# Attention passes and MLP of a transformer block written out as one list of ticks, with the row maxima placed by DMA

## The chip, the core and the metric

The kernel runs on one core of one Trainium2 chip. Five engines work side by side: TensorE (PE, matmuls into PSUM; its weight loads are shown apart as PEld), VectorE (DVE), ScalarE (ACT), GpSimd (POOL) and SyncE (SP), which issues all of the kernel's transfers. The metric is the device time in microseconds (us) from the first to the last instruction.

## The reference

Two cross-attention layers and one MLP, all in float32, over 8 batches of 512 rows and 512 columns, with 16 heads of 32 columns. The first layer's result of batch 0 is added to every batch.

```python
# layer 0
att = softmax(q @ k.T / sqrt(32)) @ v      # q of x, k and v of ctx
x = x + att[0]                             # batch 0's attention for all batches
# layer 1, for each batch
q = layer_norm(x) @ Wq;  k, v = layer_norm(ctx) @ Wkv
x = x + softmax(q @ k.T * SCALE) @ v @ Wproj + bproj
x = x + gelu(layer_norm(x) @ W1 + b1) @ W2 + b2     # hidden width 2048
```

So there are 9 attention passes: pass 0 for layer 0 (batch 0 alone) and passes 1 to 8 for the batches of layer 1.

## The kernel before

Every float32 operand of a product is held as two parts (hi and lo, in the fast type fp32r), and each product is three matmuls: hi by hi, hi by lo, lo by hi. A projected tile of 128 x 512 (a "unit") is so 12 matmuls of 512 columns for its 4 chunks of the inner dimension.

An attention pass is 64 quarters (`CH`): 16 heads, 4 chunks of 128 rows each. In quarter k the PE makes the scores of chunk k with queries as rows (`ps_s`, L587), DVE takes their row maxima (L993), and 6 quarters later (`SHIFT_LAG`) PE makes the same scores again with keys as rows (`ps_t`, L602), now with a 97th inner row that holds minus the maxima, so that they come out shifted. ACT takes the exponential twice (L806 as the hi part, L812 whole), DVE subtracts for the lo part (L999; chunk 2 of each head on POOL, L1175), and 8 quarters after the first scores (`WEIGH_LAG`) PE multiplies both parts with the values (`ps_o`, L622). The three operands of a head lie one above the other in `q_st` and `k_st`; SP stacks them with 4 transfers per head (`load_stack`, L376) and lays the head's result into place with 2 (`place_head`, L391 and L392).

How the maxima come into the 97th row of `q_st`: once a head has its 4 columns of maxima, PE spreads them with 4 small matmuls against an identity (L634), and ACT copies one row of 512 (L799):

```python
for c in range(TC):
    ins = nc.tensor.matmul(ps_m[0:KM, c * P:c * P + P],
                           negmax[:, h % 2, c:c + 1].broadcast_to([P, KM]), id_r[:], ...)
act.activation(q_st[KQ:KM, h % G], ps_m[KQ:KM], ACT.Identity).then_inc(m_moved, 1)
```

Between these, `PLAN` puts the parts of other units by quarter: the values, keys and queries of the passes next, the output projection of the pass before, the transposes of the layer norms. Passes 0, 1 and 8 are written out (`FIRST`, `COLD`, `LAST`), passes 2 to 7 are a hardware loop on every engine. When all passes are through, the MLP runs by itself, batch by batch (`tile`): hidden units (L696), Gelu twice from PSUM (L880, L881), the subtraction on DVE (L1063), and the second product (L710), which adds up over all 16 hidden units in four PSUM banks. Its weights stay in SBUF, where the attention's tiles were; the rows between the two parts go through DRAM (`x2_scratch`).

Of the kernel before, what the change touches and what calls it, by code (L numbers as in the profile page):

```python
# [11 lines left out]
P = 128  # L27
# [28 lines left out]
POOL_CHUNK = 2
STACK_AHEAD = 6  # L60

EARLY = TC
TURN_AT = 12
# [5 lines left out]
PLAN = [  # L69
    (("v", 0), 0, (4, 4, 5, 5)), (("v", 1), 1, (5, 6, 6, 6)), (("v", 2), 0, (7, 7, 7, 8)),  # L70
    (("v", 3), 1, (8, 8, 9, 9)), (("q", 1), 0, (10, 10, 11, 11)), (("k", 2), 1, (12, 13, 14, 15)),
    (("out", 0), 0, (16, 17, 17, 18)), (("out", 1), 1, (18, 19, 20, 20)), (("q", 2), 0, (21, 22, 23, 23)),
# [6 lines left out]
]  # L79


def plus(a, b):

    return a + b if b >= 0 else a - (-b)


class Pass:


    def __init__(self, n, kind="steady"):  # L90
        self.n = n
        self.first, self.cold, self.last = kind == "first", kind == "cold", kind == "last"
        self.follows = kind in ("steady", "last")
        self.quarters = CH + (DRAIN if self.first or self.last else 0)
        if self.first:
            plan = [u for u in PLAN if u[0][0] in "vyqk" and u[0] != ("q", G)]
            after = [("next v", c) for c in range(TC)] + [("out", c) for c in range(TC)]
            after += [("x", c) for c in range(FC)] + [("q", G)]
        elif self.cold:
            plan, after = [u for u in PLAN if u[0][0] not in ("v", "out")], []  # L100
        elif self.last:
            plan = [(("h", u[0][1]), *u[1:]) if u[0][0] == "x" else u for u in PLAN
                    if u[0][0] != "y" and not (u[0][0] in "qk" and u[0][1] >= G)]

            after = [("g", c) for c in range(EARLY)] + [("end", c) for c in range(TC)]
        else:
            plan, after = PLAN, []

        self.parts, self.his, self.los, filled_at, hi_at = {}, {}, {}, {}, {}
        for (kind, c), _, quarters in plan:  # L110
            for i, k in enumerate(quarters):
                self.parts.setdefault(k, []).append((kind, c, i))
            filled_at[kind, c] = hi = quarters[-1]
            free = {"q": c - 1, "k": c - 2}.get(kind, 0)
            if free > 0:
                hi = max(hi, TC * G * free + SHIFT_LAG + 2)
            hi_at[kind, c] = hi

        order = sorted(filled_at, key=filled_at.get) + after
        split = sorted((u for u in hi_at if u[0] != "out"), key=hi_at.get)  # L120
        for kind, c in split:
            self.his.setdefault(hi_at[kind, c], []).append((kind, c))
# [21 lines left out]
    def bank(self, kind, c):  # L144
        return self.banks[kind, c]
# [1137 lines left out]
```

## Time and profile before

| | |
|---|---|
| times, 3 runs | 1985.64, 1981.67, 1985.51 us, median 1985.51 |
| profiled execution, first to last instruction | 1982.7 us |
| PE, PEld busy | 1845.7, 1378.9 us |
| DVE, ACT, POOL busy | 1089.4, 1149.8, 614.8 us |
| mean granted PE clock | 0.966 of full speed |
| transfers | 153.08 MB, 27.6% of 16 DMA engines |

The profiled execution has no time of its own beside its span of 1982.7 us; the span lies 2.8 us under the median of the three runs and between their lowest and highest. A PE that is called busy is not at its peak, since a matmul of 512 columns is shown with some 0.39 us while the next one starts 0.23 us after it.

### The profile page before, as it was taken

The numbers are of one execution on the slowest core, as the hardware profiler recorded it, in microseconds if no ns is written. First come the engines' busy times: TensorE is split into PE (matmuls) and PEld (weight loads), VectorE is DVE, ScalarE is ACT, GpSimd is POOL, SyncE is SP. The second block draws the span as 40 slices with busy tenths as digits, with TensorE's granted clock in tenths as the row PEclk, the third lists the DMA queues.
The fourth block names the chain that finished last, engine by engine and source line by source line (L and its number), as shares of the span: only waits on it lengthen the run. The fifth ranks groups of instructions, "written<-read, shape, count | busy, mean of one in ns | idle before, by whom it ended". The sixth has DMA issues, their size and how long they took to land.

```text
span 1982.7 us, 26788 instructions
## 1 busy us (share of the span) xinstructions
PE 1845.7 (93%) x8064; PEld 1378.9 (70%) x8064; DVE 1089.4 (55%) x1852; ACT 1149.8 (58%) x2026; POOL 614.8 (31%) x494
## 2 busy tenths in 40 slices
PE   6986799999999999999999996899999999999999
PEld 4654466766767667666676664688888888888887
DVE  4774687877778868777787776222222222222221
ACT  3894497796886967968869777423223232323231
POOL 3451236354353453533534436540000101000000
PEclk9997799998999999989999998999999999999999
DMA  6330434343342433433424334311010110101010
GB/s 208 83 89 11 113 85 112 79 104 103 100 119 60 105 100 80 105 101 101 119 58 108 105 101 125 103 63 64 0 64 0 63 35 28 63 0 63 0 43 22
DMA packets 85981, 153.08 MB, mean 77 GB/s; under 512 B 17520, under 2 KB 17648, under 8 KB 83952
## 3 DMA queue, kind: packets, MB, share of 16 engines
q1 hardware_dynamic: 85872, 151.96, 27.6%
q14 instruction: 81, 0.66, 0.1%
q8 instruction: 28, 0.46, 0.1%
HBM read 59.33 MB, written 16.78 MB: 38 GB/s over the span
## 4 chain that ended last, share of the span: by engine, by line
PE 71%; issue 7%; ACT 7%; DVE 6%; DMA 4%; SPq 3%; POOL 2%; ACTq 0%; DVEq 0%; POOLq 0%
PE ps_d L696 17%; PE ps_d L569 15%; PE ps_s L710 9%; PE ps_o L622 9%; PE ps_t L710 9%; PE ps_t L602 5%; PE ps_s L587 4%; DMA k_st<-k_hl 3%; SPq L376 2%; ACT ps_t L812 2%; PE ps_m L634 2%; ACT p_hi L806 1%; DVE p_lo L999 1%; DVE negmax L993 1%; DVE yt L954 1%
## 5 line engine op out<-in xcount | busy, mean ns | idle before, releaser
L993 DVE TENSOR_REDUCE negmax<-ps_s 128x1 fp32r<-128x512 f32 x576 | 387.7, 675 | 55.9 <-PE ps_s L587 44.6
L806 ACT ACTIVATE p_hi<-ps_t 128x512 fp32r<-128x512 f32 x576 | 343.8, 597 | 128.2 <-PE ps_t L602 113.0
L1063 DVE TENSOR_TENSOR p_lo<-ps_d,p_hi 128x512 fp32r<-128x512 f32 x128 | 88.5, 691 | 544.8 <-ACT ps_d L881 544.8
L880 ACT ACTIVATE p_hi<-ps_d,col_s 128x512 fp32r<-128x512 f32 x128 | 88.2, 689 | 512.5 <-PE ps_d L696 512.5
L999 DVE TENSOR_TENSOR p_lo<-ps_t,p_hi 128x512 fp32r<-128x512 f32 x432 | 295.2, 683 | 110.6 <-ACT ps_t L812 110.3
L1175 POOL TENSOR_TENSOR p_lo<-p_full,p_hi 128x512 fp32r<-128x512 f32 x144 | 185.7, 1290 | 543.8 <-ACT p_full L812 543.6
L696 PE MATMUL ps_d<-xT,w_hi 128*128 128x512 f32 x1024 | 315.2, 389 | 0.0
L587 PE MATMUL ps_s<-k_st,q_st 96*128 96x512 f32 x576 | 252.9, 440 | 48.8 <-DMA k_st<-k_hl 25.0
L602 PE MATMUL ps_t<-q_st,k_st 97*128 97x512 f32 x576 | 251.2, 436 | 18.9 <-ACT q_st L799 9.1
L812 ACT ACTIVATE ps_t<-ps_t 128x512 f32<-128x512 f32 x432 | 257.9, 597 | 0.0
L622 PE MATMUL ps_o<-p_hi,v_s 128*65 128x512 f32 x576 | 241.6, 419 | 15.7 <-ACT o_raw L820 11.3
L622 PE MATMUL ps_o<-p_lo,v_s 128*65 128x512 f32 x576 | 234.1, 406 | 0.0
L696 PEld LDWEIGHTS ps_d<-xT,w_hi 128*128 128x128 f32 x1024 | 192.1, 188 | 40.1 <-DVE p_lo L1063 0.2
L696 PE MATMUL ps_d<-xT,w_lo 128*128 128x512 f32 x512 | 199.3, 389 | 0.0
L587 PEld LDWEIGHTS ps_s<-k_st,q_st 96*128 96x128 f32 x576 | 114.3, 199 | 118.8 <-DVE negmax L993 44.6
L602 PEld LDWEIGHTS ps_t<-q_st,k_st 97*128 97x128 f32 x576 | 113.5, 197 | 87.7 <-DVE p_lo L999 52.3
L1220 POOL TENSOR_TENSOR xres<-xres,b_s 128x2048 f32<-128x2048 f32 x8 | 36.8, 4601 | 397.8 <-DMA xres<-x_scratch 397.8
L569 PE MATMUL ps_d<-yT,wk_s 128*128 128x512 f32 x432 | 123.9, 401 | 2.0 <-POOL wk_s L1105 2.0
L569 PE MATMUL ps_d<-xT,wq_s 128*128 128x512 f32 x432 | 120.6, 400 | 3.0 <-DVE xT L922 2.2
L622 PEld LDWEIGHTS ps_o<-p_hi,v_s 128*65 128x65 f32 x576 | 80.5, 140 | 60.4 <-ACT o_raw L820 29.5
L799 ACT ACTIVATE q_st<-ps_m 1x512 fp32r<-1x512 f32 x144 | 85.2, 592 | 59.5 <-PE ps_m L634 55.5
L622 PEld LDWEIGHTS ps_o<-p_lo,v_s 128*65 128x65 f32 x576 | 81.3, 141 | 45.1 <-issue 3.4
(115 smaller groups left out, 3114.1 us busy)
## 6 DMA issues: line engine op xcount, KB each, us to landing
q_st<-q_hl SPq DMA_DIRECT2D x144, 128.0 KB, 2.8
k_st<-k_hl SPq DMA_DIRECT2D x144, 128.0 KB, 2.6
o_ab<-o_raw SPq DMA_DIRECT2D x144, 128.0 KB, 2.7
xt<-x SPq DMA_DIRECT2D x9, 1024.0 KB, 8.7
q_st<-q_hl SPq DMA_DIRECT2D x144, 64.0 KB, 2.2
k_st<-k_hl SPq DMA_DIRECT2D x144, 64.0 KB, 2.0
yt<-ctx SPq DMA_DIRECT2D x8, 1024.0 KB, 5.7
xres<-x SPq DMA_DIRECT2D x8, 1024.0 KB, 6.2
```

Of the source, the lines that this page charges most:

```text
L569: ins = nc.tensor.matmul(dst, lhs[a], rhs[b], start=(i == 0 and n == 0), stop=(i == FC - 1 and n == 2))
L587: nc.tensor.matmul(ps_s[:, c % 2], q_st[0:KQ, h % G, c * P:c * P + P], k_st[0:KQ, h % G], start=True, stop=True).then_inc(s_ready, 1)
L602: nc.tensor.matmul(ps_t[:, c % 2], k_st[0:KM, h % G, c * P:c * P + P], q_st[0:KM, h % G], start=True, stop=True).then_inc(t_ready, 1)
L622: ins = nc.tensor.matmul(ps_o[0:VW], v_s[:, c, h % NH], src[:, c], start=(c == 0 and n == 0), stop=(c == TC - 1 and n == 1))
L696: ins = nc.tensor.matmul(ps_d[:, c % 2], w[a][:, q, k, j * P:j * P + P], xT[:, b, k], start=(k == 0 and n == 0), stop=(k == FC - 1 and n = ...
L710: ins = nc.tensor.matmul(out_banks[k], g[a][:, c % TC, k * P:k * P + P], w[b][:, c], start=(c == 0 and n == 0), stop=(c == HC - 1 and n == 2))
L806: act.activation(p_hi[:, c], ps_t[:, c % 2], ACT.Exp, scale=SCALE)
L812: act.activation(whole, ps_t[:, c % 2], ACT.Exp, scale=SCALE).then_inc(p_exp, 1)
L993: dve.tensor_reduce(negmax[:, h % 2, c:c + 1], ps_s[:, c % 2], AX.X, ALU.max, negate=True).then_inc(s_maxed, 1)
L999: dve.tensor_tensor(p_lo[:, c], ps_t[:, c % 2], p_hi[:, c].bitcast(F32), ALU.subtract).then_inc(p_split, 1)
L1063: dve.tensor_tensor(p_lo[:, c % TC], ps_d[:, c % 2], p_hi[:, c % TC].bitcast(F32), ALU.subtract).then_inc(split["g"], 1)
L1175: pool.tensor_tensor(p_lo[:, POOL_CHUNK], p_full[:], p_hi[:, POOL_CHUNK].bitcast(F32), ALU.subtract).then_inc(p_pool_split, 1)
```

## The change

The two loops, `PLAN`, the class `Pass` and the separate MLP go away. A class `Plan` writes one list of 617 ticks that all engines follow. A tick is one chunk of attention (first scores; shifted scores of 6 ticks before; value product of 8 ticks before) with parts of other units at three places in it: behind the first scores, behind the shifted ones, and at the end.

- Pass 0 takes up the keys and values of batches 1 to 6 and part of 7; the short stretch between passes 0 and 1 (`gap`) the others' share and the first query unit; pass 1 all queries; passes 2 to 8 each the output projection of the pass before and 16 hidden and 16 second-product units of the MLP.
- Keys, queries and values go to DRAM (`k_scratch`, `q_scratch`, `v_scratch`), and are read back for every head (`load_stack`, still 4 transfers) or group of 4 heads (`load_values`). The split MLP weights go to DRAM in pass 0 (`piece`) and are read in slabs of 512 KB, 32 for each batch (`load_w1`, `load_w2`).
- Row maxima: DVE transposes the 4 columns, and SP places them with 4 transfers per head; the spreading matmuls and ACT's copy are gone.
- Gelu works on groups of 4 hidden units (a "burst"): DVE adds the bias out of PSUM into SBUF, ACT takes Gelu twice over 128 x 2048, POOL subtracts over 128 x 2048. There are 4 bursts for each batch, and the exponentials of the attention go on between them.
- The second product stays in PSUM for 4 hidden units only; DVE adds each of its 16 results per batch to the residual.
- The lo parts of the first layer's weights are made on DVE, not on POOL; each tick's quarter of units still shares the two banks `ps_d`.

```diff
+class Plan:
+    def core(self, first, last, tick):
+        for s in range(first, last):
+            at = tick + s - first
+            self.s_at[at], self.t_at[at + SHIFT], self.pv_at[at + WEIGH] = s, s, s
+    def build(self):
...
+            if old:
+                burst(at + 6, old, 2, second(old, 1)[:3])
+                spread(range(at + 7, at + 25), second(old, 1)[3:] + hidden(old, 3) + outs)
+                burst(at + 26, old, 3, second(old, 2)[:3])
+                spread(range(at + 27, at + 41), second(old, 2)[3:] + turns + hidden(new, 0))
+                burst(at + 41, new, 0, second(old, 3)[:3])
+                spread(range(at + 42, at + 55), second(old, 3)[3:] + hidden(new, 1))
...
+            burst(at + 55, new, 1, second(new, 0)[:3])
+            spread(range(at + 56, at + CH + 6), second(new, 0)[3:] + hidden(new, 2))
...
+    for h in range(NP * NH):
+        at = PLAN.tick_of_s[h * TC]
+        heads.append((max(at - STACK_AHEAD, stored), h))
+        rows.append((at + TC, h))
+        at = PLAN.tick_of_pv[h * TC + TC - 1]
+        places.append((at + (4 if h % G == 0 else 1), h))
...
 SP
+        def load_row(h):
+            sp.wait_ge(max_turned, h + 1)
+            for c in range(TC):
+                sp.dma_start(q_st[KQ:KM, h % G, c * P:c * P + P].bitcast(F32),
+                             negmax_t[c:P:32, h % 2]).then_inc(row_loaded[h % 2], 16)
+            k_hi = kd[n, own, 0].unsqueeze(1).broadcast_to([DK, 2, T])
+            for dst, src in ((q_st[0:2 * DK, k], qd[n, own]), (k_st[0:2 * DK, k], k_hi),
+                             (q_st[2 * DK:KQ, k], qd[n, own, 0]), (k_st[2 * DK:KQ, k], kd[n, own, 1])):
+        for tick in range(TICKS):
+            for h in ROWS.get(tick, []):
+                load_row(h)
+            for u in STORES.get(tick, []):
+                store(*u)
+            for h in HEADS.get(tick, []):
+                load_stack(h)
+            for h in PLACES.get(tick, []):
+                place_head(h)
...
 PE
-                    for c in range(TC):
-                        ins = nc.tensor.matmul(ps_m[0:KM, c * P:c * P + P],
-                                               negmax[:, h % 2, c:c + 1].broadcast_to([P, KM]),
-                                               id_r[:], start=True, stop=True)
+            fill(tick, 0)
+            s = PLAN.t_at.get(tick)
+            if s is not None:
+                h, c = divmod(s, TC)
+                if c == 0:
+                    pe.wait_ge(row_loaded[h % 2], 16 * ROW_DMAS * (h // 2 + 1))
...
 ACT
-                    act.activation(q_st[KQ:KM, h % G], ps_m[KQ:KM], ACT.Identity).then_inc(m_moved, 1)
-            act.activation(p_hi[:, c % TC], ps_d[:, c % 2], ACT.Gelu, bias=b1)
-            act.activation(ps_d[:, c % 2], ps_d[:, c % 2], ACT.Gelu, bias=b1).then_inc(hi_ready, 1)
+            for n, group in PLAN.bursts.get(tick, []):
+                done = GELU_NO[n, group]
+                act.wait_ge(evacuated, ready("hid", n, 4 * group + 3))
+                act.activation(g_s[:, done % 2, 0], h_st[:, done % 2], ACT.Gelu)
+                act.activation(h_st[:, done % 2], h_st[:, done % 2], ACT.Gelu).then_inc(gelu_done, 1)
...
 DVE
+                if c == TC - 1:
+                    dve.wait_ge(s_maxed, s + 1)
+                    if h >= 2:
+                        dve.wait_ge(row_loaded[h % 2], 16 * ROW_DMAS * (h // 2))
+                    dve.transpose(negmax_t[:, h % 2], negmax[:, h % 2].bitcast(F32)).then_inc(max_turned, 1)
...
+                dve.tensor_scalar(h_st[:, done % 2, c % 4], bank(u), col_s[:, 6 * FC + c:6 * FC + c + 1], None,
+                                  ALU.add).then_inc(evacuated, 1)
+            else:
+                dve.tensor_tensor(xres[n % 2][:, t], bank(u), xres[n % 2][:, t], ALU.add).then_inc(evacuated, 1)
...
 POOL
+            for n, group in PLAN.bursts.get(tick, []):
+                done = GELU_NO[n, group]
+                pool.wait_ge(gelu_done, done + 1)
+                pool.tensor_tensor(g_s[:, done % 2, 1], h_st[:, done % 2], g_s[:, done % 2, 0].bitcast(F32),
+                                   ALU.subtract).then_inc(g_split, 1)
```

## Rows read from the trace of the kernel before

**Rows 1.** The page: span, busy time of each engine, what the transfers moved.

```profile
span 1982.7 us, 26788 instructions
PE 1845.7 (93%) x8064; PEld 1378.9 (70%) x8064; DVE 1089.4 (55%) x1852; ACT 1149.8 (58%) x2026; POOL 614.8 (31%) x494
...
q1 hardware_dynamic: 85872, 151.96, 27.6%
```

**Rows 2.** Windows: 132 us of attention, 88.8 us of MLP; columns as headed.

```profile
core 0: us, PE busy (x) PEld busy (x) DVE busy (x) ACT busy (x) POOL busy (x), PEclk, DMA share, GB/s
387.00:519.00 132.00, 124.91 (x544) 88.68 (x543) 102.83 (x176) 102.53 (x188) 58.38 (x48) 0.95 0.37 97
1361.00:1449.80 88.80, 88.80 (x401) 73.60 (x400) 20.62 (x36) 24.91 (x40) 5.81 (x3) 1.00 0.11 36
```

**Rows 3.** Windows of the row-maximum line alone: pass 0, gap, one pass.

```profile
33.00:161.00 128.00, 43.02 (x64) 0.97 0.38 104
161.00:211.00 50.00, 2.28 (x4) 0.67 0.09 21
343.00:475.00 132.00, 43.13 (x64) 0.95 0.38 97
```

**Rows 4.** The chain that ended last: start, us, what.

```profile
387.67 3.46 issue
402.03 5.55 DMA k_st<-k_hl
...
1305.32 2.72 PE ps_d L696 x12
```

**Rows 5.** SyncE's timeline: two outputs' stores, one MLP batch apart.

```profile
1360.69 0.39 SPq L488 DMA_DIRECT2D out<-xres  x1
...
1449.64 0.41 SPq L488 DMA_DIRECT2D out<-xres  x1
```

**Rows 6.** Groups of instructions, whole span.

```profile
L993 DVE TENSOR_REDUCE negmax<-ps_s 128x1 fp32r<-128x512 f32 x576 | 387.7, 675 | 55.9 <-PE ps_s L587 44.6 <-issue 10.4
L806 ACT ACTIVATE p_hi<-ps_t 128x512 fp32r<-128x512 f32 x576 | 343.8, 597 | 128.2 <-PE ps_t L602 113.0 <-issue 9.9
L999 DVE TENSOR_TENSOR p_lo<-ps_t,p_hi 128x512 fp32r<-128x512 f32 x432 | 295.2, 683 | 110.6 <-ACT ps_t L812 110.3
...
L799 ACT ACTIVATE q_st<-ps_m 1x512 fp32r<-1x512 f32 x144 | 85.2, 592 | 59.5 <-PE ps_m L634 55.5
...
L634 PEld LDWEIGHTS ps_m<-id_r,negmax 128*97 128x97 f32 x576 | 74.5, 172 | 36.1 <-issue 11.7 <-DVE negmax L993 2.3
...
L1220 POOL TENSOR_TENSOR xres<-xres,b_s 128x2048 f32<-128x2048 f32 x8 | 36.8, 4601 | 397.8 <-DMA xres<-x_scratch 397.8
...
L758 ACT ACTIVATE w_hi<-xt 128x2048 fp32r<-128x2048 f32 x4 | 7.7, 1920 | 3.9 <-DMA xt<-w 3.9
```

**Rows 7.** ScalarE's timeline where Gelu follows the last exponentials.

```profile
1252.88 0.60 ACT L820 ACTIVATE o_raw<-ps_o 65x512 f32<-65x512 f32 x1 [1.49 <-PE ps_o L622]
1253.49 1.28 ACT L880 ACT_TABLE_LOAD   x1
```

**Rows 8.** SyncE's timeline: a stack's issues, a large one, the first head.

```profile
29.20 0.69 SPq L376 DMA_DIRECT2D q_st<-q_hl  x1
...
799.66 0.59 SPq L376 DMA_DIRECT2D q_st<-q_hl  x1
...
800.29 0.60 SPq L376 DMA_DIRECT2D k_st<-k_hl  x1
...
1454.15 0.38 SPq L492 DMA_DIRECT2D xres<-x_scratch  x1
```

**Rows 9.** Transfers by form: KB each, median us from issue to landing.

```profile
k_st<-k_hl SPq DMA_DIRECT2D x144, 128.0 KB, 2.6
...
yt<-ctx SPq DMA_DIRECT2D x8, 1024.0 KB, 5.7
...
rs<-o_raw SPq DMA_DIRECT2D x144, 2.0 KB, 2.2
```

**Rows 10.** Timeline: from matmul to row maximum and to exponentials.

```profile
803.69 0.39 PE L602 MATMUL ps_t<-q_st,k_st 97*128 97x512 f32 x1
...
804.61 0.59 ACT L812 ACTIVATE p_full<-ps_t 128x512 f32<-128x512 f32 x1
...
818.21 0.51 PE L587 MATMUL ps_s<-k_st,q_st 96*128 96x512 f32 x1 [0.25 <-DVE negmax L993]
...
818.67 0.68 DVE L993 TENSOR_REDUCE negmax<-ps_s 128x1 fp32r<-128x512 f32 x1
```

More of the change, by code:

```diff
@@ L82, in plus @@
[L82 to L105, printed above, removed]
-        else:
[L107 to L122, printed above, removed]
-        for kind, c in sorted(hi_at, key=hi_at.get):
-            self.los.setdefault(hi_at[kind, c] + 1, []).append((kind, c))
-        split += [u for u in after if u[0] not in ("out", "end")]
-        self.no = {u: i for i, u in enumerate(order)}
-        self.units, self.splits = len(order), len(split)
-        self.split_no = {u: i for i, u in enumerate(split)}
-        self.banks = {u: b for u, b, _ in plan}
-        self.banks.update({u: i % 2 for i, u in enumerate(after)})
-    def base(self, steady, before):
-        if isinstance(self.n, int) and self.n < 2:
-            return before[self.n]
-        return (self.n - 2) * steady + before[2]
-    def unit(self, kind, c):
-        return self.base(len(PLAN), UNITS_BEFORE) + self.no[kind, c]
-    def split(self, kind, c):
-        return self.base(len(PLAN) - TC, SPLITS_BEFORE) + self.split_no[kind, c]
-    def bank(self, kind, c):
-        return self.banks[kind, c]
-    def chunk(self, c):
-        return plus(self.n * CH, c)
-    def split_by_vector(self, j):
-        h, c = divmod(j, TC)
-        return plus(self.n * (NH * (TC - 1)), (TC - 1) * h + (c if c >= POOL_CHUNK else c + 1))
-    def head(self, h):
-        return plus(self.n * NH, h)
-    def runs(self, c):
-        return c < CH and (c >= 0 or self.follows)
@@ L165 @@
-class Before:
-    n, first = 0, True
-    order = [("y", c) for c in range(FC)] + [("x", c) for c in range(FC)] + [("k", 0), ("q", 0), ("k", 1)]
-    def unit(self, kind, c):
-        return self.order.index((kind, c))
-    split = unit
-    def bank(self, kind, c):
-        return self.unit(kind, c) % 2
-PRE_UNITS = len(Before.order)
-FIRST, COLD, LAST = Pass(0, "first"), Pass(1, "cold"), Pass(B, "last")
-UNITS_BEFORE = [PRE_UNITS, PRE_UNITS + FIRST.units, PRE_UNITS + FIRST.units + COLD.units]
@@ new lines, with listed @@
+PLAN = Plan()
+NO = PLAN.no
+TICKS = PLAN.ticks
+def listed(pairs):
+    out = {}
+    for t, x in pairs:
+        out.setdefault(t, []).append(x)
+    return out
+EVACUATED = {}
+for _u in PLAN.units:
+    _t, _p = PLAN.ends[_u]
+    EVACUATED.setdefault((_t + (_p == 2), _p == 1), []).append(_u)
+NORMS = [("y", b) for b in range(B)] + [("x", b) for b in range(B)] + [("h", n) for n in range(1, NP)]
+NORM_NO = {u: i for i, u in enumerate(NORMS)}
+KQ_NO = {u: i for i, u in enumerate(u for u in PLAN.units if u[0] in ("k", "q"))}
@@ new lines, with transposed, ready, emptied @@
+V_NO = {u: i for i, u in enumerate(u for u in PLAN.units if u[0] == "v")}
+GELU_NO = {u: i for i, u in enumerate(u for t in sorted(PLAN.bursts) for u in PLAN.bursts[t])}
+STAGED = [("y", b) for b in range(B)] + [("x", b) for b in range(1, B)]
+STAGE_NO = {u: i for i, u in enumerate(STAGED)}
+def transposed(kind, b):
+    return ("a", 2 + b if kind == "y" else 10 + b, FC - 1)
+def ready(*u):
+    return NO[u] + 1
+def emptied(*u):
+    t, p = PLAN.ends[u]
+    return t + (p == 2)
+def norm_ticks(kind, i):
+    if kind == "y":
+        at = PRE + 5 if i == 0 else PLAN.end("a", 2 + i, 0) - 6
+        return at, at + 1, at + 3
+    if kind == "x":
+        if i == 0:
+            return PLAN.gap + 2, PLAN.gap + 2, PLAN.gap + 3
+        at = PLAN.end("a", 10 + i, 0) - 6
+        return at, at + 1, at + 3
+    at = emptied("out", i, TC - 1)
+    return at, at, at + 1
@@ L738, in _, with transposes @@
[L738 to L750 removed]
+        def transposes(u, src):
+            for t in range(TC):
+                ins = nc.tensor.transpose(bank(u)[:, t * P:t * P + P], src(t), id_s[:])
+            ins.then_inc(unit_ready, 1)
@@ L962, in invert @@
+        def invert(n, g, step):
+            done = n * G + g
             if step == 0:
@@ L1120, in join @@
+        def join(n, g, step):
+            done = n * G + g
             if step == 0:
```

1610 lines of the change are left out of this document (799 added, 811 removed), and 9 rows, old and new, of tables (PLAN, raw_in).

## The prediction

> **What bounds the kernel now.** I read the page first [rows 1]: PE counts as busy for 93% of the span, DVE, ACT and POOL for at most 58%. That busy is not work at full pace, so the second view is the windows [rows 2]. In the MLP PE is busy without a gap while DVE and ACT stand idle for over 70%; in an attention pass DVE and ACT are each busy for 103 of 132 us. The two halves of the kernel have opposite idle engines. The windows of the row-maximum line [rows 3] give the stages: pass 0 takes 128 us, the gap behind it 50 (4 maxima, clock 0.67), and each pass of 64 maxima 132.
>
> PE's own price comes from the chain: 12 matmuls of 512 columns in 2.72 us, 0.2267 each [rows 4]. One MLP batch, 384 such matmuls and 16 transposes, takes 88.95 us between two stores [rows 5]: 87.05 for the matmuls, so 0.12 for a transpose. A pass holds 256 matmuls of attention and 192 of projections (101.6 us), 32 transposes (3.8) and 64 spreading matmuls (about 8, from their weight loads' 74.5 us over 576 [rows 6]): 113.4 us of work in 132.1. Of the 18.7 us lost, 3.5 are an issue gap in each round of the loop and 5.6 the wait for a stack transfer right after it [rows 4]; 9.6 are spread over the quarters. So attention is bound by PE with delays from its neighbours on top, the MLP by PE alone.
>
> **The change, counted in PE work.** The list in the diff can be counted. It keeps 7056 matmuls of 512 columns (1599.6 us) and 432 transposes (52) and drops 576 spreading ones: 1652 us where the kernel before needs about 1721. The rest, 260 us before, is what can be won or lost again. By stages, work by the two prices:
>
> - Up to the first scores: 33 us before. The first stack's issue begins at 29.2 [rows 8]; now the first keys and queries go to DRAM (an issue, and 2.6 to land, as a 128 KB stack has [rows 9]) and are read from there: 37.
> - Pass 0, first 10 ticks: 138 matmuls, 31.3; I take 36. The other 62: 814 matmuls and 112 transposes, 197.7; with the 5% that evenly spread delays cost a pass in which one tick lasts 3.2 us: 207.
> - Gap: 144 matmuls, 48 transposes, 38.3. The wait for the last query to go out to DRAM and come back as a stack (some 8 us, of which two units cover 5.4) and the joins make 45. Before: 50.
> - Pass 1: 576 and 96, 141.9, taken as 150. Pass 2: 559 and 32, 130.5; its first burst has nothing put beside it, so ACT's 6.4 us (below) show: 142.
> - Passes 3 to 8: 688 and 16, 157.8 each, six times.
> - What follows (8 ticks of attention, then MLP only): 673 and 16, 154.4, taken as 160, since each burst there lies beside a group of 48 matmuls (10.9 us).
>
> **A steady pass (3 to 8), engine by engine.** DVE: 64 maxima at 0.675 and 48 subtractions at 0.683 [rows 6] are 76; 40 evacuations of units at 0.68 another 27; inverting, layer norm and 16 small transposes some 18: 121 of 158, 77%, as before. ACT: exponentials 128 x 0.597 and 16 moves at 0.59, 86 us; the copy of the maxima (16 x 0.592) is gone. Four bursts come in. Gelu over 128 x 2048 out of SBUF has no row; the nearest is the copy of that shape, 1.92 [rows 6], and 0 is excluded, since every column passes the engine. With Exp and Gelu in turn, each burst has two table loads; the one row has 1.28 [rows 7]. 2 x 1.92 + 2 x 1.28 = 6.4 us a burst. Beside it PE has 3 second-product units put in front of its shifted scores, 8.16 us. So bursts are hidden, 6.4 against 8.16; without that cover each costs PE about 6. POOL's subtraction of that shape is put at its addition's 4.6 [rows 6] and is due a whole group of ticks later: hidden.
>
> The Trainium skill (ScalarE: Activation LUTs, What ACT_TABLE_LOAD costs) has 1.38 us of drain at every switch beside the load. The load in rows 7 starts 0.01 us after the move before it ends, so the trace shows none. By that page of the Trainium skill a burst is 9.2 us, about 1 over its cover, and the whole sum would be up to 30 us more.
>
> **SP is the engine to watch.** A stack's transfers are issued 0.64 us apart (0.60 each, with the step between them), large plain ones cost 0.38 [rows 8]. Before, a head costs 6 issues, 3.8 us of 8.3. Now it costs 10 (4 stack, 4 maxima, 2 placing), 6.4 us. A steady pass adds 38 others, most of them slabs, at some 0.45. That is 160 x 0.64 + 38 x 0.45 = 119 us of 158, but a burst's tick is 9 us long and gives SP little to do. Between bursts a tick has on average 1.98 us of PE work, so 7.9 for a head, against 6.4 + 1.1 = 7.5 on SP. In two of the four stretches (ticks 42 to 54 and 56 to 5) I count 27 us of issues against 25 and 26 of PE work. SP works strictly in order and waits at its own entries: a maximum's transfer can stand behind a placing that waits for POOL's join, and behind the stacks of the head after.
>
> **The new chain.** From the fourth scores of a head at X: the maximum starts 0.46 later [rows 10] if DVE is free. It is not: the subtraction of the tick before waits for exponentials that end 1.5 us behind their matmul [rows 10], so the maximum ends at about X + 1.5 and the small transpose (no row; between 0 and the 0.7 of a full one, taken as 0.25) at 1.75. Four issues: the last starts at 3.7; landing 2.2, as the 2 KB transfer has it [rows 9]: X + 5.9. The old way needed only PE and ACT. The shifted scores follow 3 ticks and one filling behind X: in ticks of 0.907 (4 matmuls) plus 3 or 6 filling ones that is 6.3 us for 5 of the 16 heads, 6.8 for 3, 7.7 for 4 and over 9 for those that span a burst. So at a landing of 2.2 nearly all fits, at 3.5 five heads stall for about 1 us each. The queue is fuller than before: a pass moves 29 MB instead of 12.6, which by the shares in rows 2 (0.37 for 97 GB/s; 0.11 for 36 where transfers are large) keeps the 16 engines busy for about 55%. A 1 MB transfer takes 5.7 [rows 9], so a slab ahead may add 1 to 2.
>
> I take 3 us for the new chain, 5 for SP's two tight stretches and 3 for the rest: 11 us, 169 for a pass (before: 9.6 lost in a denser one, and the loop's 9.1 are gone, since nothing loops). Both ends: 4 us lost (162), if the chain and SP are hidden; 24 lost (182), if each of the 16 heads loses a further 0.8.
>
> **Sum.** 37 + 36 + 207 + 45 + 150 + 142 + 6 x 169 + 160 = 1791, and 3 for the last store: span 1794. Before the span lay 2.8 under the median, so 1797 us, 9.5% less. Where it is won, in short: 69 of PE work, about 60 of loop gaps with their waits, and some 60 by filling pass 0, the gap and the way into the MLP.
>
> **Rivals.**
> *All hidden.* DVE and ACT are no fuller than before, and four heads of a pass have a burst to hide in. Passes at 162 and 12 less elsewhere: 1797 - 42 - 12, about 1743. Against it: SP at 95% between bursts.
> *SP becomes the bound.* Stretches follow SP and the placing's waits. Passes at 182, passes 1 and 2 each 10 more: 1797 + 78 + 20 = 1895.
> *Slower: maxima by DMA.* If the four transfers land in 5.9 instead of 2.2 (behind slabs and stacks; a 1 MB load's figure), the chain is 9.6 long and 12 of 16 heads stall, 5 for 3.3, 3 for 2.8 and 4 for 1.9: 33 us a pass instead of 3. Stalls also delay SP's later entries. Steady passes near 200, passes 1 and 2 near 190 and 183: 1797 + 186 + 40 + 41 = about 2060. It decides from a landing of about 5 on. Against it: the 2 KB transfer of before lands in 2.2, right behind one of 128 KB.
> *No change:* only as a chance meeting between the last two.
>
> **Chances.** Forecast 0.46, all hidden 0.17, SP the bound 0.20, slower 0.15, no change 0.02. What this measurement can tell from no change is about 0.2%, 4 us: faster 0.83, same 0.02, slower 0.15. The forecast's own range is 1765 to 1845. The range for 8 in 10 leaves out nearly all of the slow rival, and the lower half of the hidden one: 1730 to 1950. PE's work alone sets a floor near 1652 + 37.
>
> **What would show it.** Right: steady passes of 64 maxima in 165 to 175 us; PE waiting for the row transfers for under 100 us in all; no PE wait for ACT near a Gelu; table loads x65 at 1.28; the row transfers at about 2.2 to 3 to landing; no window as idle as the gap at clock 0.67. Wrong: PE's idle ahead of the shifted scores put down to those transfers for over 200 us, landings of 4 and more, SP's issues longer than 0.64 under the fuller queue, which I have no row for, or a clock below 0.95 in the steady passes, as every stall that lets it fall costs twice.

## The result and the profile after

The changed kernel is slower: 2107.49 us median of 4 runs (2095.91 to 2111.21) against 1985.58 (1981.67 to 1985.98) before, ratio 1.061, 95% interval 1.058 to 1.064. The forecast was 1797. The profiled execution has a span of 2103.3 us.

The page of the changed kernel, the lines that answer to [rows 1, 6], with its chain by line and two kinds of transfer (KB each, us to landing):

```profile
span 2103.3 us, 23386 instructions
...
PE 1804.3 (86%) x7488; PEld 1368.4 (65%) x7488; DVE 1242.5 (59%) x2100; ACT 1093.0 (52%) x1728; POOL 728.6 (35%) x481
...
q1 hardware_dynamic: 156256, 353.16, 55.0%
...
PE ps_d L805 43%; PE ps_o L854 9%; DMA q_st<-negmax_t 5%; PE ps_t L837 5%; PE ps_s L822 5%; DVE ht L1026 2%; SPq L574 2%; SPq L569 2%; DVE stats L1008 2%; DVE negmax L1065 1%; DVE p_lo L1078 1%; DVE stage L1026 1%; ACT ps_t L922 1%; ACT p_hi L916 1%; ACT ps_d L870 1%
...
L1175 POOL TENSOR_TENSOR g_s<-h_st,g_s 128x2048 fp32r<-128x2048 f32 x32 | 147.8, 4618 | 174.9 <-ACT h_st L907 174.9
...
w_r<-w_scratch SPq DMA_DIRECT2D x256, 512.0 KB, 5.4
```

Less work on PE, as counted, but 86% busy where it was 93%. What it waits for stands in the view of waits of PE (us in total, times, longest):

```profile
PE ps_t L837 <- DMA q_st<-negmax_t: 87.0, 25, 8.4
PE ps_d L805 <- DVE kq_out L950: 32.6, 22, 4.0
PE ps_d L805 <- DVE v_out L950: 31.5, 24, 4.4
PE ps_d L805 <- DVE xres_b L988: 27.1, 4, 8.2
PE ps_d L805 <- DVE xres_a L988: 24.6, 3, 8.2
```

Three causes, then: row maxima that land late, units' results that DVE takes late out of the two banks (`kq_out`, `v_out`), and a stall of 8.2 us, about once a pass, for DVE at the residual (`xres`). The windows, cut where each pass's first row maximum starts (startup; pass 0 with the gap; passes 1, 2 and 3; then 4 to 7), show where they sit:

```profile
0.00:36.20 36.20, 15.69 (x58) 12.24 (x59) 16.27 (x18) 12.42 (x14) 0.34 (x6) 0.79 0.68 239
36.20:392.00 355.80, 296.64 (x1256) 225.52 (x1256) 206.81 (x366) 171.86 (x289) 112.14 (x86) 0.95 0.66 230
392.00:594.00 202.00, 165.62 (x678) 121.70 (x679) 147.68 (x273) 116.96 (x206) 83.36 (x70) 0.92 0.57 183
594.00:756.00 162.00, 142.41 (x592) 104.59 (x591) 110.44 (x190) 104.64 (x176) 65.56 (x42) 0.95 0.49 143
756.00:947.00 191.00, 168.17 (x703) 127.59 (x702) 117.95 (x196) 108.24 (x168) 70.23 (x43) 0.96 0.54 154
947.00:1719.00 772.00, 677.00 (x2818) 513.71 (x2818) 473.22 (x785) 433.62 (x673) 280.73 (x172) 0.94 0.55 154
```

| stage | forecast | measured | PE idle | granted clock |
|---|---|---|---|---|
| startup | 37 | 36 | | 0.79 |
| pass 0 and gap | 288 | 356 | 59 | 0.95 |
| pass 1 | 150 | 202 | 36 | 0.92 |
| pass 2 | 142 | 162 | 20 | 0.95 |
| passes 3 to 8, each | 169 | 193 (3 to 7: 192.5) | 23.6 (3 to 7) | 0.94 |
| the rest | 163 | 189 | 21 | 0.93 |

For passes 3 to 7 the table closes: the work of the forecast's own prices, divided by the granted clock, plus the idle time gives 157.8 / 0.94 + 23.6 = 191.5. The forecast had 11 us for all losses; so two things are missing in each steady pass, about 13 us of idle time and 10 us of clock. For pass 0 with its gap the same sum gives 267.3 / 0.95 + 59 = 340 and for pass 1 141.9 / 0.92 + 36 = 190; the 16 and 12 us that are left to the measured 356 and 202 are not explained here.

**One late row.** A head's maxima are turned by DVE at 1091.63, in 0.21 us. Until the row's first issue SP is at other work (its timeline), and the last of the four transfers lands 6.54 us after its issue (the chain of waits; the line below it is PE's own timeline):

```profile
1091.98 0.43 SPq L569 DMA_DIRECT2D k_st<-k_scratch  x1
1092.46 0.46 SPq L660 DMA_DIRECT2D w_r<-w_scratch  x1
1093.02 0.62 SPq L585 DMA_DIRECT2D o_ab<-o_raw  x1
1093.68 0.59 SPq L586 DMA_DIRECT2D rs<-o_raw  x1
1094.32 0.58 SPq L650 DMA_DIRECT2D w_r<-w_scratch  x1
1094.94 0.45 SPq L660 DMA_DIRECT2D w_r<-w_scratch  x1
1095.43 2.19 SPq L574 DMA_DIRECT2D q_st<-negmax_t  x4
```

```profile
1097.13 6.54 DMA q_st<-negmax_t
1103.67 0.04 issue
1103.71 0.79 PE ps_t L837
...
1103.71 0.79 PE L837 MATMUL ps_t<-q_st,k_st 97*128 97x512 f32 x1 [6.93 <-DMA q_st<-negmax_t]
```

The row is issued 3.6 us late, behind the end of a stack, a placing and three slabs of 512 KB. In SP's program the rows stand first in their tick and the slabs last, so all of this belongs to ticks before, with which SP is not through. The row then lands in 6.5 us instead of 2.2 [rows 9]. PE idles 6.93 us. And then it works at a granted clock of 0.50, the lower of the two levels, 1.2 instead of 2.4 GHz, with the DMA engines full (windows of the 5 us after it, and of 24 us before it without a large stall):

```profile
1103.00:1108.00 5.00, 4.29 (x10) 3.21 (x11) 1.55 (x3) 1.56 (x3) 0.00 (x0) 0.50 1.04 241
960.00:984.00 24.00, 24.00 (x106) 18.75 (x104) 12.44 (x21) 15.25 (x21) 12.25 (x7) 1.00 0.37 103
```

This is one of the long waits, not the usual row. In passes 3 to 7 PE waited for 14 of 80 rows, for 63.7 us in all. In passes 3 to 8 SP issued the first transfer of half of the rows within 0.03 us of their turning, and only 13 of 95 waited over 1 us for it (longest 4.25). The trace shows a landing only where somebody waited for it, so the landings named here are those of late rows.

**One stall for the residual.** The layer norm of the MLP's input runs on DVE in one piece, just while POOL is at its long subtraction (timelines of DVE and POOL):

```profile
1018.85 2.46 DVE L1008 BATCH_NORM_STATS2 stats<-xres_b 128x6 f32<-128x512 f32 x4
...
1023.25 6.95 DVE L1026 TENSOR_SCALAR ht<-xres_b,mv,rstd 128x512 f32<-128x512 f32 x4 [1.48 <-POOL rstd L1131]
1030.12 0.68 DVE L1065 TENSOR_REDUCE negmax<-ps_s 128x1 fp32r<-128x512 f32 x1
1030.73 1.27 DVE L988 TENSOR_TENSOR xres_a<-ps_d,xres_a 128x512 f32<-128x512 f32 x2
```

```profile
1024.34 4.67 POOL L1175 TENSOR_TENSOR g_s<-h_st,g_s 128x2048 fp32r<-128x2048 f32 x1
```

Sum and length are different things here: four scalings of 0.53 each alone are 2.1 us of DVE, but DVE is gone for 11 us in a row (2.46, a wait of 1.48 for POOL, 6.95), and the evacuation that PE waits for comes behind them. The longest single scaling of the norms takes 4.71 us, as long as POOL's instruction.

### The profile page after: what moved, and what is told of

Its sections match the earlier page's. It is cut to its first block, busy times and chain, and to the rows that moved or that the text cites. A ratio compares the mean times of both kernels' runs of the same rounds, so it can differ in the third digit from the quotient of the medians.

```text
span 2103.3 us, 23386 instructions
## 1 busy us (share of the span) xinstructions
PE 1804.3 (86%) x7488; PEld 1368.4 (65%) x7488; DVE 1242.5 (59%) x2100; ACT 1093.0 (52%) x1728; POOL 728.6 (35%) x481
## 4 chain that ended last, share of the span: by engine, by line
PE 62%; DVE 10%; DMA 8%; SPq 6%; ACT 5%; issue 4%; POOL 4%; DVEq 1%; POOLq 0%; ACTq 0%
PE ps_d L805 43%; PE ps_o L854 9%; DMA q_st<-negmax_t 5%; PE ps_t L837 5%; PE ps_s L822 5%; DVE ht L1026 2%; SPq L574 2%; SPq L569 2%; DVE stats L1008 2%; DVE negmax L1065 1%; DVE p_lo L1078 1%; DVE stage L1026 1%; ACT ps_t L922 1%; ACT p_hi L916 1%; ACT ps_d L870 1%
## 5 line engine op out<-in xcount | busy, mean ns | idle before, releaser
L805 PE MATMUL ps_d<-hT,w_r 128*128 128x512 f32 x1536 | 445.1, 407 | 7.7 <-DVE hT L950 7.7
L805 PE MATMUL ps_d<-w_r,g_s 128*128 128x512 f32 x1536 | 391.6, 404 | 56.0 <-DVE xres_b L988 27.1
L805 PEld LDWEIGHTS ps_d<-w_r,g_s 128*128 128x128 f32 x1536 | 299.8, 196 | 128.2 <-DVE xres_b L988 28.8
L805 PEld LDWEIGHTS ps_d<-hT,w_r 128*128 128x128 f32 x1536 | 302.2, 197 | 89.5 <-DVE hT L950 10.7
L822 PE MATMUL ps_s<-k_st,q_st 96*128 96x512 f32 x576 | 237.1, 412 | 14.0 <-DMA k_st<-k_scratch 10.8
L1175 POOL TENSOR_TENSOR g_s<-h_st,g_s 128x2048 fp32r<-128x2048 f32 x32 | 147.8, 4618 | 174.9 <-ACT h_st L907 174.9
L805 PE MATMUL ps_d<-aT,wk_s 128*128 128x512 f32 x384 | 114.5, 421 | 33.6 <-DVE v_out L950 31.5
L805 PE MATMUL ps_d<-aT,wq_s 128*128 128x512 f32 x384 | 118.4, 423 | 28.7 <-DVE kq_out L950 28.2
L981 DVE TENSOR_SCALAR h_st<-ps_d,col_s 128x512 f32<-128x512 f32 x128 | 94.1, 735 | 42.6 <-PE ps_d L805 42.1
L805 PE MATMUL ps_d<-wo_s,oT 128*128 128x512 f32 x384 | 109.5, 401 | 7.8 <-POOL oT L1155 7.0
L805 PEld LDWEIGHTS ps_d<-aT,wk_s 128*128 128x128 f32 x384 | 74.7, 201 | 59.6 <-DVE v_out L950 39.4
```

The lines of the kernel that those rows point to most:

```text
L805: ins = nc.tensor.matmul(bank(u), lhs[a], rhs[b], start=(i == 0 and m == 0), stop=(i == 3 and m == 2))
L822: nc.tensor.matmul(ps_s[:, c % 2], q_st[0:KQ, h % G, c * P:c * P + P], k_st[0:KQ, h % G], start=True, stop=True).then_inc(s_ready, 1)
L981: dve.tensor_scalar(h_st[:, done % 2, c % 4], bank(u), col_s[:, 6 * FC + c:6 * FC + c + 1], None, ALU.add).then_inc(evacuated, 1)
L1175: pool.tensor_tensor(g_s[:, done % 2, 1], h_st[:, done % 2], g_s[:, done % 2, 0].bitcast(F32), ALU.subtract).then_inc(g_split, 1)
```

## The experiments

Ratios are to the kernel before, timed on the same chip, with 95% intervals; the changed kernel's is 1.061 (1.058 to 1.064). "Steady" is a pass of passes 3 to 7.

**1. Maxima by TensorE and ScalarE again.** PE's spreading matmuls and ACT's copy come back; they need a PSUM bank, so the attention's results have one instead of two.

```diff
-            for h in ROWS.get(tick, []):
-                load_row(h)
+                for c in range(TC):
+                    ins = nc.tensor.matmul(ps_m[0:KM, c * P:c * P + P],
+                                           negmax[:, h % 2, c:c + 1].broadcast_to([P, KM]), id_r[:], ...)
...
+                act.activation(q_st[KQ:KM, h % G], ps_m[KQ:KM], ACT.Identity).then_inc(m_moved, 1)
```

> Undoes one part alone: the row maxima are spread by PE's 4 small matmuls and copied by ACT again, with one PSUM bank for the value product instead of two; all else is the changed kernel. Changed kernel: 2107 us, span 2103, PE idle 87 us ahead of the shifted scores for the row transfers. Theory A (the row transfers land late because weight slabs and stacks stand ahead of them on SP's queue, and every such stall also lets PE's clock fall): stalls of 87 and roughly 50 of clock go, 576 small matmuls cost about 65 of PE: 2030 to 2060. Rival B (DVE's lumps, four layer-norm operations in one tick, are what costs, the row stalls only stand in front of them): no gain, the small matmuls show in full, 2110 to 2170. Rival C (taking up the MLP under the passes costs more than that by itself: PSUM banks, transfers, ACT's table loads): between the two, but with steady passes still over 185 us.

2037.72 us, ratio 1.027 (1.022 to 1.032). The waits for rows are gone and a steady pass takes 181.5 us instead of 192.5 (granted clock 0.98), although PE does more. It is not back at the kernel before: the waits for `v_out`, `kq_out` and `xres` stand unchanged (33.5, 30.1, 52.1 us).

**2. Slabs only right behind rows.** The two lists of slab loads are moved to the tick after a row's.

```diff
+    def behind(pairs):
+        return [(max(t, min(t + (1 - t) % 4, PLAN.base[NP] - 4)), x) for t, x in pairs]
+    first, second = behind(first), behind(second)
```

> Keeps the row maxima on DMA, but SP issues the MLP's weight slabs only in the tick right behind a row entry, so that no slab stands ahead of the rows; same transfers, same bytes, same number of issues. Theory A (what stands ahead on the queue): rows land in under 3.5 us instead of 4.9 to 6.5, PE's idle for them falls from 87 to under 25 us, 2010 to 2050 us in all. If instead SP's issue time (4 issues for the rows, 10 for a head) is what makes them late: no change, 2095 to 2110. Rival B (DVE's lumps): 2080 to 2110, and the idle moves to evacuations.

2078.38 us, ratio 1.048 (1.043 to 1.053). Steady 187; the waits for rows fall from 87.0 to 64.4 us. A row now has no slab of the ticks just before it ahead of it on SP; the longest wait of a row in SP's queue falls from 4.25 to 2.77 us. But the late ones still land 2.4 to 7.0 us after their issue in passes 3 to 8. The slabs issued some 5 to 8 us earlier can still be under way then: they take 5.5 us in the median, up to 9.6.

**3. Rows issued by ScalarE.** The four transfers go out on ACT's own queue, ahead of its work of the tick.

```diff
+            for h in ROWS.get(tick, []):
+                act.wait_ge(max_turned, h + 1)
+                for c in range(TC):
+                    act.dma_start(q_st[KQ:KM, h % G, c * P:c * P + P].bitcast(F32), negmax_t[c:P:32, h % 2])
```

> The four row transfers of a head are issued by ACT on its own queue, at the same tick; slabs stay where they are. It takes 576 issues (318 us) off SP and puts them on ACT. Theory A in its queue form (order on SP's queue is what counts): rows land in under 3.5 us, idle for them under 25, 2010 to 2060. If the 16 DMA engines are simply full at those moments, another queue helps less: landing 4 to 5, 2070 to 2100. If ACT's 2.3 us of issues per head delay its exponentials and evacuations: 2090 to 2130, with new PE waits for ACT.

2078.84 us, ratio 1.048 (1.040 to 1.056), steady 185.5. The waits for rows are 46.5 us. Here no other transfer stands before a row on its queue, and it still lands late: in the chain of waits of this kernel

```profile
817.48 5.02 DMA q_st<-negmax_t
926.05 4.39 DMA q_st<-negmax_t
935.42 3.99 DMA q_st<-negmax_t
```

The middle line is the row of head 59 in pass 3. The same row lands in 6.57 us in the changed kernel, in 4.39 here and in 1.92 without slabs (run 7). So some 2.2 us of it went with sharing a queue with the slabs and 2.5 with their traffic as such; the slabs are not issued at quite the same moments in these kernels, so the division is rough. The Trainium skill says (DMA: Bandwidth & Descriptors, "Issuing engines are not separate DMA queues") that transfers started by different engines run on the same 16 DMA engines and interleave. The 4.39 against 1.92 agrees.

**4. The norm's work one operation a tick.** Statistics and scalings go out one a tick, the loads and sums they need 3 ticks earlier.

```diff
-            for t in range(TC):
-                ins = dve.tensor_scalar(dst[:, t], src[:, t], mv[:, no % 2, t, 0:1], rstd[:, no % 2, t:t + 1],
+            dve.tensor_scalar(dst[:, t0], src[:, t0], mv[:, no % 2, t0, 0:1], rstd[:, no % 2, t0:t0 + 1],
```

> The layer norm's four statistics and four scalings stand one to a tick on DVE instead of four in one tick (but for the first two of the keys' inputs and the first ones of the queries and of the MLP, whose place leaves no room); its loads and sums are issued 3 ticks earlier. Rival B (DVE's lumps hold up the evacuation of units, so PE waits for a bank): PE's idle for DVE before matmuls of units falls from some 140 us to under 50, 1990 to 2040 us. Theory A (rows are the main cost): the 8.2 us wait of each steady pass gets shorter, the row stalls stay: 2040 to 2080. If it is POOL's long subtraction that holds DVE's scaling up (four scalings took 6.95 us beside it), the spreading alone leaves that wait: 2070 to 2100.

2064.48 us, ratio 1.041 (1.035 to 1.047), steady 185.5. The stall for `xres` in five steady passes falls from 42.5 to 5.1 us, but 9.0 us of waits for the scaled rows themselves (`ht`) are new; waits for rows of maxima stay (62.5). Pass 1 gets longer, 219, as DVE there waits at its earlier statistics for POOL's sums (31.2 us instead of 2.5).

**5. Weight of the short units.**

```diff
-COST = {"a": 2.0, "tg": 2.0, "ht": 2.0}
+COST = {"a": 8.0, "tg": 2.0, "ht": 2.0}
```

> One number is changed: the planner's weight of a unit of four transposes (the a units) from 2 to 8, so that fewer ticks separate it from its neighbours' banks being free. Theory (short units starve the banks in passes 0 and 1): in the changed kernel TensorE idles 38.5 us for v_out and kq_out in passes 0 with its gap and 26.6 us for kq_out in pass 1; with the unit weighing as much as its evacuation takes, half to three quarters of the 65 us go, and the time falls by 30 to 50 us to about 2057 to 2077; passes 3 to 8 stay at 191 to 194 us each. Rival (passes 0 and 1 are bound by the DMA share, 0.78 in pass 0, or by the engines' own sums): the waits move to another releaser and the time stays within 10 us of 2107.

2092.78 us, ratio 1.058 (1.055 to 1.061), which overlaps the changed kernel's interval. The waits for `v_out` and `kq_out` in passes 0 and 1 fell from 71 to 60 us, not by half or more. So the short units are at most a small part of it.

**6. POOL's long operations in four.**

```diff
+                for c in range(4):
+                    ins = pool.tensor_tensor(g_s[:, done % 2, 1, c], h_st[:, done % 2, c],
+                                             g_s[:, done % 2, 0, c].bitcast(F32), ALU.subtract)
```

> GpSimd's two long operations (the subtraction of 128x2048 at 4.62 us and the addition of the second bias) are each issued as four of 128x512, the same work. Theory (VectorE's scaling of the layer norm is held up for the whole of GpSimd's instruction): the longest scaling falls from 4.71 us to below 2, the stall of TensorE on the norm's result of 8.2 us in each steady pass falls to 4 or 5, and the time falls by 15 to 30 us to 2077 to 2092. Rival (the two engines share the port in turn, whatever the length of an instruction): the four scalings together still take about 7 us while GpSimd works, the stall stays at 8 us and the time within 10 us of 2107, or above it by the extra issue costs.

2096.22 us, ratio 1.060 (1.052 to 1.067): no difference that this can measure. What it tells is in the scalings, the changed kernel first, then this one (number of instructions, min/median/max in ns):

```profile
L1026 DVE TENSOR_SCALAR ht<-xres_a,mv,rstd x12: 533/972/4711, 831.4 to 1608.6; 128x512 f32<-128x512 f32 x12
```

```profile
L1026 DVE TENSOR_SCALAR ht<-xres_a,mv,rstd x12: 1409/1478/1482, 842.2 to 1610.9; 128x512 f32<-128x512 f32 x12
```

The two engines take turns by instruction: no scaling is held for 4.7 us any more, but those beside POOL's work are each held for about one piece of POOL's (1.3 us). Four take 5.6 instead of 7.0, and the stall 6.9 instead of 8.2. Both expectations were half right. The Trainium skill has a rule for this (SBUF — State Buffer, "Who interferes with whom"): when VectorE works in one of its two-port modes, which `tensor_scalar` can enter, it and GpSimd contend for a shared pair of ports, and whoever issues first holds it for the whole instruction. The trace agrees, 4.71 us against POOL's 4.67.

**7. No later slabs.** Only the first batch's slabs are loaded; the later batches multiply what lies in the buffers, so this kernel leaves out work and serves the measurement alone. With the transfers their issues on SP are gone too.

```diff
+            if i >= 4:
+                return
```

> The weight slabs of the MLP (512 KB each) are loaded for the first batch only, and the later batches multiply whatever slab is in the buffer: the loads of passes 3 to 8 are left out of the computation, the instructions of the other engines are the same. Theory (row maxima land late since they stand behind slabs and stacks in the same queue): landings fall from 4.9 to 6.5 us towards the 2.2 to 2.6 us of a quiet queue, the 12.9 us of row stalls in each steady pass go to below 4, and with the clock that comes back a steady pass takes 172 to 180 instead of 192.5: time 2000 to 2030. Rival (the placing of rows is slow by itself, 4 issues of 0.56 us and a landing, whatever traffic is beside it): row stalls of 8 us and more a pass stay and the time is above 2065.

1995.19 us, ratio 1.010 (1.007 to 1.012), the largest effect of one edit: 17 us in each steady pass (192.5 to 175.5, granted clock 0.98). PE's waits:

```profile
PE ps_t L840 <- DMA q_st<-negmax_t: 8.1, 11, 1.6
```

and the landings of the rows in the chain of waits:

```profile
894.79 1.92 DMA q_st<-negmax_t
1071.20 1.52 DMA q_st<-negmax_t
```

Passes 0 and 1, which have next to no slabs either way, are hardly changed (362 and 198 against 356 and 202). In the steady passes the placing by itself costs little; placing beside 32 slabs of 512 KB a pass does.

**8. No Gelu.** `ACT.Identity` in place of `ACT.Gelu`, so no table is changed; the output is another function's.

> The Gelu of the MLP is an Identity, so that ScalarE never changes its table (53 loads of 1.28 us are gone, 67.9 us of ScalarE) and the output is another function's. Theory (the bursts of Gelu with their table loads lie behind TensorE's matmuls, as no wait of TensorE stands at them in the trace): the time stays within 15 us of 2107. Rival (the bursts delay the exponentials and so the chain): each of the 26 bursts gives 2.6 us or more back, time 2040 or below.

2099.46 us, ratio 1.061 (1.054 to 1.069): no effect. The bursts are hidden.

**9. One tick more.**

```diff
-SHIFT = 6
-WEIGH = 8
+SHIFT = 7
+WEIGH = 9
-STACK_AHEAD = 6
+STACK_AHEAD = 5
```

> The shifted scores follow the first scores by 7 ticks instead of 6 and the value products by 9 instead of 8, and stacks are asked for 5 ticks ahead instead of 6; nothing else. A tick is about 2 us between bursts. Theory (row maxima land 2 to 7 us too late and nothing else is wrong with them): each stall behind them is about 2 us shorter, 77.4 us of row stalls in passes 3 to 8 fall to 40 to 55, and the time by 25 to 45 us, to 2062 to 2082. Rival (SyncE's queue is full, so that whatever is given to the rows is taken from the stacks, which are asked for one tick later): the stalls move to the stacks and the time stays within 10 us of 2107 or goes above it.

2043.1 us, ratio 1.031 (1.029 to 1.033), more than was expected: 2 us of room bring 10 us a steady pass (183). The waits for rows go from 87.0 to 28.3 us while the late rows still land as late (4.4 to 7.9 us in its chain of waits); for stacks there is no new wait (10.7 us, before 10.8).

**10, 11. Two combinations.** Edits 9, 2, 3, 4, 5 and 6 together, and edits 9, 1, 4, 5 and 6 together.

> Six edits together, the maxima still placed by DMA: lag of 7 ticks, slabs only right behind rows, rows issued by ScalarE, the norm's statistics and scalings one per tick, GpSimd's long operations in four, the a units weighed 8. Theory (stalls of rows and of the norm are separate and nearly add): alone against the changed kernel slabs gave 1.4%, rows by ScalarE 1.3%, the norm 2.1%, units and pieces 0.5%; the first two cure the same stall, so that 4 to 5% in all is left, a ratio to the kernel before of 1.010 to 1.025, about 2000 to 2030 us. Rival (each stall hides another, as DMA landings are late for whoever comes): ratio above 1.035. A gain over the kernel before needs passes 0 and 1 shorter too, for which there is nothing in it but the norm.

1951.9 us, ratio 0.984 (0.982 to 0.987): faster than the kernel before, and than was expected. Steady passes take 171 us, PE's waits for rows 2.3 us in all.

> Maxima spread by TensorE and copied by ScalarE again, with the norm's work one operation a tick, GpSimd's long operations in four, the a units weighed 8, and the lag of 7 ticks. By stages: startup 36, pass 0 with its gap 350, pass 1 205, pass 2 163, passes 3 to 8 at 172 (181.5 with the maxima on TensorE alone, less the 8.3 us a pass that it idled for the norm), tail 170: 1956 us. Theory (the placing by DMA and the lumps of the norm are what loses): ratio to the kernel before 0.98 to 1.00. Rival (the list of ticks is slower by itself, whatever the stalls): ratio 1.01 and more.

1963.32 us, ratio 0.991 (0.989 to 0.993). Steady passes 174. So the list of ticks wins either way once most of its stalls are gone, and with enough lag the maxima by DMA are slightly the cheaper way, with the slabs moved for them.

**12. Three banks for the units.** Passes 0 and 1 were still 339 and 202 in run 10 (the 205.6 in the expectation of run 13 is not what its trace has). The third bank is taken from the attention's results.

```diff
-    ps_o = nc.alloc_psum_tensor("ps_o", [P, 2, T], F32)
-    ps_d = nc.alloc_psum_tensor("ps_d", [P, 2, T], F32)
+    ps_o = nc.alloc_psum_tensor("ps_o", [P, T], F32)
+    ps_d = nc.alloc_psum_tensor("ps_d", [P, 3, T], F32)
```

> The units beside the attention rotate over three PSUM banks instead of two; the third is taken from the attention's results, which now have one bank instead of two. Weights of the a units are as in the changed kernel. Theory (in passes 0 and 1 a unit waits since VectorE comes late to the bank of two units before, with lumps and waits of its own ahead of it in its order): the waits for v_out, kq_out and aT, 50.6 us in pass 0 with its gap and 28.7 in pass 1, fall by more than half, to below 40 in all; passes 3 to 8 gain 0 to 5 us each, since the wait for the norm's result is not one for a bank; time 2040 to 2065. Rival (VectorE is behind by its own sum, and more banks only move the wait to the next one, or the single bank of results brings a wait for ScalarE's move): the waits stay above 60 us or reappear at ps_o, time within 15 us of 2107.

2019.24 us, ratio 1.019 (1.017 to 1.021), 4% off the changed kernel with a bank only moved. Pass 0 with its gap takes 327 instead of 356, pass 1 189 instead of 202, a steady pass 187 instead of 192.5. In passes 0 and 1 the waits for `v_out`, `kq_out` and `aT` fall from 80 to 23 us, while those for rows and for DVE's row maxima grow from 7 to 30; what is won there is less idle time by 31 us. The stall for `xres` is also shorter, 4.6 instead of 8.2, which the expectation had ruled out: the unit that waited there waited for a bank as well.

**13. Three banks on run 10.**

> The six edits of the run at 0.984 with the three banks added. Theory (late evacuations in passes 0 and 1): pass 0 with its gap falls from 338.5 to about 322, pass 1 from 205.6 to about 185, the steady passes stay at 168 to 170; ratio to the kernel before 0.960 to 0.972. Rival (the waits move, as above): ratio 0.980 or more.

1952.28 us, ratio 0.985 (0.983 to 0.987): nothing gained. Passes 0 and 1 are shorter (317 and 196), steady passes longer (176), for a wait has taken the place of the old ones (view of waits of PE):

```profile
PE ps_o L863 <- ACT o_raw L945: 88.3, 95, 3.7
```

The single bank of results must be empty before the next head's products, and ACT moves it out only behind its four row issues (ACT's timeline):

```profile
1000.74 2.09 ACTq L913 DMA_DIRECT2D q_st<-negmax_t  x4
1002.93 0.60 ACT L930 ACTIVATE p_hi<-ps_t 128x512 fp32r<-128x512 f32 x1 [2.18 <-PE ps_o L863]
1003.43 0.59 ACT L936 ACTIVATE ps_t<-ps_t 128x512 f32<-128x512 f32 x1
1003.94 0.59 ACT L945 ACTIVATE o_raw<-ps_o 65x512 f32<-65x512 f32 x1
```

**14. The same, rows issued by SyncE again** (edits 9, 2, 4, 5, 6 and 12).

> The last combination with one edit taken back: the row transfers are issued by SyncE again. So it has the lag of 7 ticks, slabs right behind rows, the spread norm, GpSimd's long operations in four, the a units weighed 8, and three banks for the units with one for the attention's results. Theory (in the last run TensorE waited 78 us in passes 1 to 7 for ScalarE's move of the results out of the single bank, since ScalarE issues four transfers, 2.09 us, ahead of it): those waits fall below 10 us, pass 0 with its gap stays at 317, pass 1 goes to 185, pass 2 to 163, steady passes to 170: ratio to the kernel before 0.955 to 0.97, about 1905 us. Rival (the rows issued by SyncE land as late as before, and give back what the waits for ScalarE took): row stalls over 25 us in passes 3 to 8, ratio 0.98 or more.

1892.07 us, ratio 0.955 (0.954 to 0.957). The wait for `o_raw` is 2.8 us, that for rows 8.9. The windows of this kernel (pass 0 with the gap, passes 1, 2 and 3, then 4 to 7):

```profile
34.00:352.00 318.00, 285.74 (x1259) 223.09 (x1258) 209.72 (x367) 170.02 (x289) 118.06 (x90) 0.95 0.75 261
352.00:546.00 194.00, 161.42 (x672) 120.70 (x671) 140.76 (x269) 114.84 (x206) 78.18 (x66) 0.91 0.55 180
546.00:700.00 154.00, 141.40 (x592) 104.64 (x592) 111.18 (x194) 103.12 (x173) 65.82 (x51) 0.96 0.49 153
700.00:867.00 167.00, 163.31 (x706) 125.74 (x705) 115.88 (x197) 108.22 (x168) 72.70 (x59) 0.99 0.58 177
867.00:1543.00 676.00, 656.39 (x2818) 502.97 (x2817) 463.57 (x785) 432.82 (x672) 290.61 (x233) 0.99 0.58 175
```

The counts of matmuls are those of the changed kernel; with the stalls gone the clock came back, from 0.94 to 0.99 in passes 3 to 7. Pass 1 is left at 194, with 32 us idle: PE waits there for POOL's subtraction (15.8 us in all, longest 6.8) and for DVE's row maxima (13.9), which was not followed up.

## Why the prediction was wrong

**The step that failed first** is "landing 2.2, as the 2 KB transfer has it". Some three rows in each steady pass lie up to 4.25 us on SP's queue and land, all but one, in 4.1 to 7.9. A 2 KB transfer among stacks says nothing of one among 512 KB slabs. The text had the number for it: a share of 55% for the DMA engines was forecast and is what was measured. This mean is made of stretches at 0.37 and at 1.0, and the late rows fall into the latter: between issue and landing the share was 0.78 to 1.04 in all but two of the 18 waits from pass 3 on.

The slower rival, "maxima by DMA", named this wait, with a landing of 5.9, and had a chance of 0.15, since the nearest row, not the fuller queue, was made to decide. But that its pass of 200 us lies near the 192.5 is in good part luck: it had 12 of 16 heads stall, 33 us a pass in all. Measured are about 3 heads a pass, 4.5 us each, 12.7 us; the rest of the loss is DVE's order and the clock, which it did not have.

**3 us for the new chain** should have been 12.7: that is what PE idled for rows in each of passes 3 to 7 (63.7 us in five).

**What was not in the sum at all** is DVE's order. The passage "inverting, layer norm and 16 small transposes some 18" counted it by its sum, as part of 121 us of 158. Put in one tick, beside POOL's long instruction, the norm's operations made a stall of 8.2 us in a pass, 42.5 in five; run 4 took 37 of them away and brought 9 back elsewhere. In passes 0 and 1 units waited for two banks; "the 5% that evenly spread delays cost" and the like, 21 us in pass 0 with its gap and 8 in pass 1, were 59 and 36 us of idle time. Run 12 shows that a third bank takes most of the waits for evacuations (80 to 23 us), which fits a DVE that is late now and then, not behind; that the same lumps make it late there was not tested.

**The clock** was named at the end as what costs twice, and not priced. Prices were taken at clock 1.00 [rows 2, 4]; the steady passes had 0.94. Those 10 us a pass went with the stalls: the clock was 0.98 in run 7 and 0.99 in run 14.

**The signs were badly set.** PE's waits for rows of "under 100 us in all" were to show the forecast right, over 200 wrong; they were 87 with the forecast 17% off. Two others served: landings of 4 and more, and a clock below 0.95.

**What held:** startup (37, measured 36), PE's work by count (7488 matmuls and transposes), DMA at 55%, the small transpose (0.25 taken, 0.21), POOL's subtraction (4.6 taken, 4.62), a burst of 6.4 us (2 x 1.28 for the tables, 1.92 and 1.90 for Gelu) hidden behind PE's 8.16, which run 8 confirms. By an estimate from the drain that the Trainium skill has (ScalarE: Activation LUTs, "What ACT_TABLE_LOAD costs") a burst would stand about 1 us out of its cover. The trace has no such drain: a load starts within 0.02 us of the end of the activation before it, and Gelu right behind the load. SP's row issues take 0.51 us in the median, not 0.60, but SP holds things up in places, as the second rival had it: 3.6 us in the row above, and 6% of the chain that ended last.

**Reached by another kernel:** run 14, with six more edits, has 168.6 us for a steady pass, where the forecast had 169 for a plan with nearly all stalls hidden. The terms are not quite the same, so the nearness is part luck: of the 11 us that the forecast gave away, 4.7 are idle time and 2 the clock, and 4 are in neither. From its 1892 to the 1797 of the forecast it is passes 0, 1 and 2 (30, 45 and 11 us) and the stretch behind the last maximum (178 against 163), less 8 us at the start and in passes 3 to 8.

## What to carry to other kernels

A small transfer on the critical path takes the landing time of the traffic that it will lie beside: compute what share of the DMA engines the new transfers take where it lies, and before anything else give it a tick more of lag, which brought 10 us a pass here. For an in-order engine look at the longest run of operations between two things that others wait for, not at its sum, and put no long GpSimd operation beside VectorE's SBUF work. When units wait for evacuation though the evacuating engine is 60% busy, try a third buffer: here it was worth 4%, the better order 2%.

## What the runs showed of the hardware

- Late rows of 0.5 KB, those that something waited for, in passes 3 to 8: without slabs they landed in 1.5 to 2.3 us, beside them in 4.1 to 7.9 (two in 2.4 and 2.8 with the DMA engines at 0.4), on ACT's queue in 2.6 to 6.4.
- A DVE scaling from SBUF to SBUF of 128x512 took 0.53 us alone, up to 4.71 while POOL worked on 128x2048, and 1.41 to 1.48 beside pieces of 128x512.
- Four issues by ACT took 2.09 us, and ACT did nothing else in them; by SP 2.2.
- In passes 3 to 8 of the changed kernel the granted clock of the 5 us after each stall of 6.8 us or more was 0.50 to 0.68, that after waits for rows under 2 us 1.00, as in the 24 us without a large stall.
